# A transformer block of three stages on one core: the length penalty added by TensorE in PSUM, one maximum over four banks, exponentials out of PSUM, and ranks by a difference and one compare

## The reference

```python
# part 1, per batch: self attention, then cross attention over a context of 2048 rows
Q = x @ Wq2
K, V = (context @ Wk2, context @ Wv2)
energy = einsum('bqd,bkd->bqk', Q, K)
lengths = sum(energy[:, 0] != 0, axis=-1)       # how many keys the first query does not meet with 0
pad = arange(2048) >= lengths
energy = where(pad, -inf, energy)
score = softmax(energy / sqrt(32), axis=-1)
# ... then a two-layer feed-forward, a layer norm after each step
# part 2: an RWKV step over the two batches
# part 3, per batch: attention with gates
gl_v = (x @ Ws).reshape(b, t, h, e)              # 8 heads, 5 experts
wv = topk_mask(gl_v, 2) * sigmoid(gl_v)          # the two highest; the lower index wins a tie
xv = einsum('btd,edk->btek', x, Wv)
v = einsum('bthe,btek->bhtk', wv, xv)
# ... softmax(q k) v, gated by topk_mask(x @ Wd, 2), through Wo
```

## Time and profile before

| | |
|---|---|
| median of 3 runs | 277.52 us (277.33 to 278.31) |
| span of the profiled execution | 275.8 us |
| PE busy | 237.3 us, 86% of the span |
| DVE busy | 177.9 us, 64% |
| ACT busy | 88.3 us, 32% |
| POOL busy | 99.6 us, 36% |
| chain that ended last | PE 54%, DVE 29%, POOL 5%, issue 5%, ACT 4% |

### The profile page before, as it was taken

How to read it: one execution, slowest core, us unless ns; L and a number is a source line. 1 busy time by engine, 2 the same in 40 slices (tenths; PEclk the granted TensorE clock), 3 DMA queues, 4 the chain that set the end, 5 groups by cost and what they waited for, 6 DMA issues and landing times.

```text
span 275.8 us, 3044 instructions
## 1 busy us (share of the span) xinstructions
PE 237.3 (86%) x1133; PEld 167.4 (61%) x1133; DVE 177.9 (64%) x327; ACT 88.3 (32%) x151; POOL 99.6 (36%) x82
## 2 busy tenths in 40 slices
PE   6999869899599949999989999970987599996995
PEld 5969458789488727677554444430433279895952
DVE  2236953379658999540747559599646869899360
ACT  2106410363467538412014545410202302321110
POOL 4002810088039933530402024886215236160000
PEclk9999968999899997999999999997799979999579
DMA  6999991002799991009800797000000000000001
GB/s 269 394 421 450 409 422 76 1 0 101 289 429 421 421 424 51 0 11 392 358 2 1 221 421 311 1 0 0 0 0 0 2 0 0 4 0 0 2 37 40
DMA packets 6350, 43.98 MB, mean 159 GB/s; under 512 B 832, under 2 KB 832, under 8 KB 1472
## 3 DMA queue, kind: packets, MB, share of 16 engines
q1 hardware_dynamic: 6336, 43.80, 39.1%
HBM read 43.27 MB, written 0.52 MB: 159 GB/s over the span
## 4 chain that ended last, share of the span: by engine, by line
PE 54%; DVE 29%; POOL 5%; issue 5%; ACT 4%; DMA 1%; DVEq 0%; POOLq 0%; ACTq 0%
PE psum L378 50%; PE psum L382 4%; DVE ring_r L809 4%; ACT slots L1338 3%; POOL small L1576 3%; DVE slots L1078 3%; DVE slots L904 2%; POOL slots L1585 2%; DVE slots L1081 2%; DVE small L785 1%; DVE slots L978 1%; DVE slots L909 1%; DMA slots<-xin 1%; DVE small L1091 1%; DVE slots L998 1%
## 5 line engine op out<-in xcount | busy, mean ns | idle before, releaser
L378 PE MATMUL psum<-ring,slots 128*128 128x512 f32 (+3 forms) x228 | 96.2, 576 | 4.4 <-ACT slots L1338 4.4
L378 PEld LDWEIGHTS psum<-ring,slots 128*128 128x128 f32 (+1 forms) x228 | 43.2, 209 | 48.7 <-issue 41.5
L1338 ACT ACTIVATE slots<-psum 128x512 f32<-128x512 f32 (+3 forms) x51 | 27.7, 552 | 123.6 <-PE psum L378 76.2
L1581 POOL TENSOR_TENSOR ring_r<-ring,ring_r 128x640 fp32r<-128x640 f32 x16 | 41.5, 2608 | 48.5 <-ACT ring_r L1338 48.5
L378 PE MATMUL psum<-slots,ring 128*128 128x128 f32 x448 | 54.7, 283 | 2.9 <-ACT slots L1338 2.4
L378 PEld LDWEIGHTS psum<-slots,ring 128*128 128x128 f32 x448 | 53.5, 199 | 5.1 <-ACT slots L1338 3.4
L378 PE MATMUL psum<-ring_r,slots_r 128*128 128x512 f32 x192 | 48.4, 410 | 3.4 <-issue 3.4
L378 PEld LDWEIGHTS psum<-ring_r,slots_r 128*128 128x128 f32 x192 | 37.1, 196 | 12.6 <-issue 4.9
L1576 POOL TENSOR_TENSOR small<-small,mhalf 128x1 f32<-128x1 f32 x16 | 14.9, 932 | 62.2 <-DVE small L789 62.2
L1338 ACT ACTIVATE ring_r<-ring 128x2048 fp32r<-128x2048 f32 (+1 forms) x17 | 31.7, 1864 | 14.2 <-PE psum L378 12.6
L382 PE MATMUL psum<-ident,slots 128*128 128x128 f32 x104 | 17.1, 298 | 19.5 <-DVE slots L1274 7.9
(11 more groups left out here) (149 smaller groups left out, 211.1 us busy)
## 6 DMA issues: line engine op xcount, KB each, us to landing
ring<-blocks SPq DMA_DIRECT2D x36, 1024.0 KB, 10.2
bc<-vecs SPq DMA_DIRECT2D x1, 3072.0 KB, 28.4
bc<-vecs SPq DMA_DIRECT2D x1, 1280.0 KB, 8.1
slots<-xin SPq DMA_DIRECT2D x2, 256.0 KB, 3.9
bc<-vecs SPq DMA_DIRECT2D x1, 512.0 KB, 9.9
y<-slots SPq DMA_DIRECT2D x2, 256.0 KB, 2.0
colv<-cols SPq DMA_DIRECT2D x1, 14.0 KB, 8.7
```

Of the source, the lines that this page charges most:

```text
L378: return t.matmul(o_, l, r, start=first, stop=last)
L1338: return a.activation(o, x, func, **kw)
L1581: g.tensor_tensor(ring_r[:, p, CUT:], ring[:, p, CUT:], ring_r[:, high(name), CUT:], ALU.subtract).then_inc(*split_lowg.inc(name))
```

## The change

- The penalty is no longer a 128x512 tile for each bank. `penalty(b)` on VectorE makes one 4x512 tile (one row for each bank, from an index that counts on over the rows and the length in PSUM), and `shut_out(b)` on TensorE adds it to the four banks with four matmuls of a 4x128 picker.
- `count2` adds the four counts up in one PSUM column: four matmuls of one column each, where there was one of four columns.
- `maxima` is one reduction over the four banks and one scaling.
- `exp2` is two exponentials of 1024, read from PSUM; in batch 1 both stand ahead of `gathered(0)`, where two stood behind `split("c12")`.
- `k2_split(1)` moves ahead of `maxima(0)`; `guard` moves to directly behind the penalty.
- `ranks` is a difference and one compare with a tie threshold (0, or minus the smallest normal number); GpSimd's `ties` is gone.
- The start-up constants change (index, picker and tie threshold for thresholds, `top` and triangle), and ScalarE copies the picker first of all. A bias row is multiplied by a 1x128 row of ones, where it was a 128x128 tile with one row of ones.

```diff
             def count2(b):
                 bk = 3 if b else 7
-                s.wait_ge(*counted[b].at("3"))
-                count(b, psum[:, bk, 0:4], cnt4[b][0:1, :], "n2")
+                for n in range(4):
+                    s.wait_ge(*counted[b].at(str(n)))
+                    i = mm(psum[:, bk, 0:1], ones[0:1, :], cnt4[b][0:1, n:n + 1], n == 0, n == 3)
+                i.then_inc(*prod[b].inc("n2"))
+
+            def shut_out(b):
+                s.wait_ge(*counted[b].at("pen"))
+                s.wait_ge(*sel_a.at("pick"))
+                for n in range(4):
+                    i = t.matmul(bank(4 * b + n), pick_r[:, n, :], pen_r[b], start=False, stop=True,
+                             skip_group_check=True)
+                i.then_inc(*shut[b].inc("pen"))
...
             def turn_p(b, n):
-                s.wait_ge(*exped[b].at(str(n)))
-                if n < 2:
-                    s.wait_ge(*maxed[b].at(str(n)))
-                else:
+                s.wait_ge(*exped[b].at(str(n // 2)))
+                if n > 1:
...
             k2(1)
+            shut_out(0)
             scores(1, 0)
...
             gather(0, 1)
+            shut_out(1)
             gather(0, 2)
...
-            def length2(b):
+            def penalty(b):
                 s.wait_ge(*prod[b].at("n2"))
...
+                s.wait_ge(*normed[b].at("x1"))
+                v.tensor_scalar(pen_r[b], kidx4[:, :], psum[0:4, 3 if b else 7, 0:1], NEG, ALU.is_ge,
+                                ALU.mult).then_inc(*counted[b].inc("pen"))
+                guard(b, psum[:, 3 if b else 7, 0:1])
 
             def maxima(b):
...
+                s.wait_ge(*shut[b].at("pen"))
+                v.tensor_reduce(mxp[b], psum[:, 4 * b:4 * b + 4, :], AX.XY, ALU.max).then_inc(*maxed[b].inc("max"))
+                s.wait_ge(*maxed[b].at("max"))
+                v.tensor_scalar(nb2[b], mxp[b], -SC, None, ALU.mult).then_inc(*maxed[b].inc("nb2"))
...
-                v.tensor_tensor(r1, other, mine, ALU.is_equal).then_inc(*gates_v[b].inc("eq"))
-                v.tensor_tensor(r0, other, mine, ALU.is_gt).then_inc(*own_v.inc())
-                s.wait_ge(*own_v.now())
-                s.wait_ge(*rank_g[b].at("tri"))
-                v.tensor_tensor(r0, r0, r1, ALU.add).then_inc(*own_v.inc())
+                s.wait_ge(*const.at("tie"))
+                v.tensor_tensor(r0, other, mine, ALU.subtract).then_inc(*own_v.inc())
+                s.wait_ge(*own_v.now())
+                v.tensor_tensor(r0, r0, tie[:, :, :].unsqueeze(1).broadcast_to([128, 16, 5, 5]),
+                                ALU.is_gt).then_inc(*own_v.inc())
...
             low("ct12")
-            length2(0)
+            penalty(0)
+            k2_split(1)
             maxima(0)
-            k2_split(1)
-            neg_max(0)
-            guard(0, len2[0])
             weigh2(0)
...
             low("c02")
-            length2(1)
+            penalty(1)
             low("c03")
             maxima(1)
-            neg_max(1)
...
+            def exp2(b, q):
                 s.wait_ge(*maxed[b].at("nb2"))
-                act(e, e, ACT.Exp, bias=nb2[b], scale=SC, accum_out=sm2[b][:, n:n + 1]).then_inc(
-                    *exped[b].inc(str(n)))
+                act(Em[b][:, q * 1024:(q + 1) * 1024].rearrange("p (n k) -> p n k", n=2),
+                    psum[:, 4 * b + 2 * q:4 * b + 2 * q + 2, :], ACT.Exp, bias=nb2[b], scale=SC,
+                    accum_out=sm2[b][:, q:q + 1]).then_inc(*exped[b].inc(str(q)))
...
             split("c12")
-            exp2(1, 2)
-            exp2(1, 3)
             copy_turned(0, "pc", T16, 3)
...
-            g.memset(top[:, :], 0.0).then_inc(*own_g.inc())
+            g.iota(kidx4[:, :], pattern=[[1, 512]], base=0, channel_multiplier=512,
+                   allow_small_or_imprecise_dtypes=True).then_inc(*const.inc("kidx4"))
+            g.memset(pick, 0.0).then_inc(*own_g.inc())
             s.wait_ge(*own_g.now())
-            g.memset(top[0:1, :], 1.0).then_inc(*const.inc("top"))
+            g.affine_select(out=pick, in_=pick, compare_op=ALU.not_equal, fill=1.0, base=0,
+                            pattern=[[-1, 4], [0, 128]], channel_multiplier=1).then_inc(*const.inc("pick"))
```

More of the change, by code:

```diff
@@ L151, in vec @@
             return bc[:, i if i < FIRST_BC else i - FIRST_BC, :]
+        pick = slots[0:4, 36, :].rearrange("p (n m) -> p n m", n=4)
+        pick_r = slots_r[0:4, 37, :].rearrange("p (n m) -> p n m", n=4)
+        pen_r = [slots_r[0:4, 34 + b, :] for b in range(2)]
         X = [slot(0), slot(1)]
@@ L198, in build @@
         lo1, re1, gd = (cells(1) for _ in range(3))
[L199 removed]
+        cnt4, len2, mxp, nb2, sm2, s1, rv2 = (cells(n) for n in (4, 1, 1, 1, 2, 1, 1))
         ss, sbs, mu8, ssq, rs8 = (cells(8) for _ in range(5))
@@ L229, in build @@
         k2_low = flags("k2_low", ["k2"])
-        counted = flags("counted", four + ["len2"])
-        maxed = flags("maxed", four + ["nb2"])
+        counted = flags("counted", four + ["pen"])
+        maxed = flags("maxed", ["max", "nb2"])
         p_low = flags("p_low", four)
@@ L246, in build @@
                       ["q1", "v1", "q2", "k2", "pc", "relu", "k", "th", "w", "r", "v", "g"])
-        exped = flags("exped", ["e1"] + four)
+        exped = flags("exped", ["e1", "0", "1"])
         split_high = Flag(sem("split_high"), SPLITS)
@@ L275, in build @@
         score = flags("score", four)
+        shut = flags("shut", ["pen"])
         p_turn = flags("p_turn", four)
@@ L400, in bias @@
             def bias(name, bk):
-                s.wait_ge(*const.at("top"))
-                mm(bank(bk), top[:, :], vec(name), True, False)
+                mm(bank(bk), ones[0:1, :], vec(name)[0:1, :], True, False)
             def natural(b, name, src, bk, what, width=512, on_bias=False):
@@ L890, in nonzero @@
                                 ALU.add, accum_out=cnt4[b][0:1, n:n + 1]).then_inc(*counted[b].inc(str(n)))
-            def length2(b):
+            def penalty(b):
                 s.wait_ge(*prod[b].at("n2"))
[L894 to L897, removed]
-            def maxima(b):
[L900 to L905, removed]
-                    s.wait_ge(*own_v.now())
-                    if n:
-                        s.wait_ge(*maxed[b].at(str(n - 1)))
-                    v.tensor_tensor_reduce(out=Em[b][:, at_], in0=bank(4 * b + n), in1=PT[b][:, at_], scale=1.0,
-                                           scalar=mxp[b][:, n - 1:n] if n else NEG, op0=ALU.add, op1=ALU.max,
-                                           accum_out=mxp[b][:, n:n + 1]).then_inc(*maxed[b].inc(str(n)))
-            def neg_max(b):
-                s.wait_ge(*maxed[b].at("3"))
-                v.tensor_scalar(nb2[b], mxp[b][:, 3:4], -SC, None, ALU.mult).then_inc(*maxed[b].inc("nb2"))
+                s.wait_ge(*const.at("kidx4"))
+                s.wait_ge(*normed[b].at("x1"))
+                v.tensor_scalar(pen_r[b], kidx4[:, :], psum[0:4, 3 if b else 7, 0:1], NEG, ALU.is_ge,
+                                ALU.mult).then_inc(*counted[b].inc("pen"))
+                guard(b, psum[:, 3 if b else 7, 0:1])
+            def maxima(b):
+                s.wait_ge(*shut[b].at("pen"))
+                v.tensor_reduce(mxp[b], psum[:, 4 * b:4 * b + 4, :], AX.XY, ALU.max).then_inc(*maxed[b].inc("max"))
+                s.wait_ge(*maxed[b].at("max"))
+                v.tensor_scalar(nb2[b], mxp[b], -SC, None, ALU.mult).then_inc(*maxed[b].inc("nb2"))
             def p_split(b, n):
@@ L1202, in _ @@
             p_split(1, 1)
-            guard(1, len2[1])
             low("c12")
@@ L1423, in fk_out, with pickers @@
                 act(bcols(T16, b), quarters(4 * b), ACT.Copy).then_inc(*gates_a[b].inc("k"))
+            def pickers():
+                s.wait_ge(*const.at("pick"))
+                act(pick_r, pick, ACT.Copy).then_inc(*sel_a.inc("pick"))
             def select():
@@ L1476, in _ @@
             out(1, "k2", bcols(T12_r, 1), quarters(6))
-            for n in range(4):
-                exp2(0, n)
+            exp2(0, 0)
+            exp2(0, 1)
             split("ct13")
```

44 lines of the change are left out of this document (15 added, 29 removed).

## The result

| | before | after |
|---|---|---|
| median of 4 runs each, one chip | 277.42 us (275.56 to 278.31) | 268.41 us (267.33 to 269.15) |
| profiled execution, span | 277.5, 275.8 us | 268.02, 266.3 us |
| share of the chain, PE and DVE | 54% and 29% | 68% and 17% |

The ratio is 0.9676, with a 95% interval of 0.9617 to 0.9735: faster by 9.0 us, where 10.5 were forecast. The range (265 to 273) and the forecast's own range (265 to 269) both hold the time. A ratio leaves out executions over 1.5% above their kernel's fastest (a slower state), so where ratio and medians differ, the ratio is the one to read. As will be seen, the mechanisms of the sum came true, but one term that it puts at nothing is not nothing, and part of the nearness is luck.

What follows compares the result with a forecast made beforehand. TensorE's chain (54%) was taken to bound the kernel, with stalls of 3.00, 4.28 and 2.69 us and a lowered clock. Span 275.8 - 4.9 (scores) - 1.4 (ranks) - 4.2 (clock) = 265.3, median 1.7 above: 267.0 us, range 265 to 273.

Steps and rivals of the forecast that it cites:

- bias products: Start-up change: one-row bias products have as many columns as the 128-row ones, so they cost nothing.
- Batch 0 and 1: Scores: PE's stalls of 3.00 and 4.28 us shrink, turn_p(0, 0) 2.3 us and gather(1, 0) 4.5 sooner; 4.9 in all.
- Rival 2: Batch 1's stall stays as GpSimd's lows come late, costing 2 to 3 us: 269.5, or 273.7 without the clock; chance 0.14.
- Ranks: Batch 1's ranks on VectorE: two dependent operations take 1.22 us in place of 2.60, so turn_max(1) comes 1.4 us sooner.
- Clock of the last part: From turn_max(1) on: idle ahead falls from 2.69 to 1.25 us, the clock stays up, 19.8 us become 15.3; 4.2 counted.
- Rival 1: The last part's clock falls all the same, from VectorE's gap and the small products behind it: 271.2 us; chance 0.25.
- Rivals 3: The scores' change gives nothing, the saved time being a wait on something else; only 1.4 from ranks: 276.0 us; chance 0.05.
- rival 4: Slower: a contraction over 4 rows takes several passes, up to 7.4 us for a shut_out: 283.7 us; chance 0.04.

Runs made afterwards that it cites:

- before_row: The kernel before with only its bias products changed, to contract one row in place of 128: 280.44 us against 276.88, ratio 1.0122.
- after_top: The kernel after with only the bias products taken back to 128 rows: 266.39 us against 276.88 for before, ratio 0.963.
- scores_top: The kernel after with the old ranks and the 128-row bias products of before: 272.63 us against 277.44 for before, ratio 0.9858.
- ranks_only: The kernel before with only the new ranks: 270.93 us against 276.88, ratio 0.9776.
- best: The kernel after with 128-row bias, one four-column count product, split("c11") behind batch 1's exponentials, v2(0) ahead of gather(1, 1): 264.23 us against 277.44 for before.
- before_fill: The kernel before with eight unused 128 x 128 products in front of turn_max(1): 272.36 us against 277.44, ratio 0.9821.
- scores_only: The kernel after with the ranks of before: 275.10 us against 276.88 for before, ratio 0.9894.
- rows_stream: The kernel after with unused 512-column fp32 products at its end, 16 each over 128, 1, 4, 32, 64, 128 rows; run once: 398.16 us.
- rows_mixed: The kernel after with unused 512-column fp32 products at its end, 16 each over 128, 64, 128, 96, 128, 32, 128 rows; run once: 372.85 us.

## Why the prediction was right, and where it was not

The lead of after over before on PE, in the profiled executions, says which term of the sum came true. After was 1.35 us ahead at the first count (64.37 against 65.72 in the earlier trace rows), before any part of the change has begun to work: the idle ahead of the products at 36 us was 2.24 us and not 3.09, and behind it the clock was low for 3.4 us and not 6.8. The other traces show that this is scatter between executions and not the change: with the start of before, the first count stands at 64.08 (before_row), 65.18, 65.25 and 65.27 us, and with the start of after at 64.11 (after_top), 64.77, 65.16, 65.34, 65.43 and 65.54. It is taken off in the first two rows.

| step | forecast | measured |
|---|---|---|
| turn_p(0, 0) sooner, from the first count | 2.3 us | 2.16 (74.22 against 77.73, less 1.35) |
| gather(1, 0) sooner, likewise | 4.5 | 4.00 (101.22 against 106.57, less 1.35) |
| four banks' maximum, exponential of 1024 | 2.3, 1.15 | 2.28, 1.11 |
| count2, shut_out | 1.1, 0.95 | 1.05, 1.19 |
| bias products | nothing | 8.83 against 7.13 us behind them |
| lead at fg(1) | 4.9 | 3.26 (231.38 against 234.64), 1.35 of it from the start |
| from fg(1) to turn_max(1) | 1.4 | 1.43 |
| from turn_max(1) to PE's last matmul | 4.2 | 4.81 (14.99 against 19.80) |
| span | 10.5 | 9.5, with the 1.35 |

**Batch 0 and 1.** Right in mechanism and nearly in size. The clock was kept over gaps of 0.34 and 0.57 us as foreseen, and the long stalls went. The half microsecond missing in batch 1 is the count and shut_out, which the sum had at 1.6 us more than before. The count now holds PE for 0.98 us from its start to the next (87.05 to 88.03), where it held it for 0.31 (90.55 to 90.86 in before); and gather(0, 1) to gather(0, 3) with shut_out between them take 9.80 us (88.03 to 97.83), where before's 36 matmuls, without a break, took 8.45. That is 2.0 us more. That GpSimd holds such operations was in the forecast (1.8 us), and the trace agrees: 1.79 for the penalty and 1.15 for the 128 x 1 product. The Trainium skill, "SBUF — State Buffer", section "Who interferes with whom", has VectorE locked out by GpSimd's use of a shared port pair when it reads two operands in SBUF, which fits the product, or works in a two-port mode; of the penalty's mode no row tells. Neither was on the path. Rival 2, a stall that stays, is out: the gap at 98.27 is 0.44 us.

**"The bias products have as many columns as before: nothing."** This is the step that failed. The four passes themselves take 1.98 us against 1.88, but the clock falls 1.4 us behind their end (at 143.5) and costs 1.7 us there; the one edit alone made the kernel before 3.4 us slower in before_row. I had counted columns and looked for the clock only where PE stands, as in the earlier trace rows. The step is wrong even though two of five traces escape the fall.

The lead of after falls from 5.99 us at the last gather (116.61 against 122.60) to 3.26 at fg(1), and 1.7 of these 2.7 us are lost behind the bias products. The rest are changes of the clock behind gaps that the change did not touch, and they go both ways. After's clock rises sooner behind the long gap at 180 us (its lead grows from 3.98 us at 188.52 to 4.63 at 198.61), and is low for longer at 215 to 222: fg(0) takes 5.70 us where it took 4.57. No run isolates these two. This is a second thing that the sum had at nothing: it carries a lead to the end unchanged. In scores_top 1.9 us of the 4.85 were lost behind such gaps.

**Ranks.** Right: 1.43 us to turn_max(1).

**Clock of the last part.** Right: the idle is 1.27 us (forecast 1.25), and the clock stays. Rival 1, a fall in spite of the short gap, is out: in all six traces with an idle of 1.27 us there, after, ranks_only, after_top and best among them, the clock stays up. That it is the idle and not the ranks, before_fill shows. The size is 0.6 us more than forecast, since I held back a wait on ACT that did not come.

**Rivals 3 and 4.** The scores do give something without the ranks, 2.9 us in scores_only and 3.9 in scores_top, each with an interval clear of nothing. A matmul over 4 rows costs 0.30 us and not the 1.1 from which rival 4 would have decided.

So the nearness of the forecast is in part luck. In the span of the profiled execution (9.5 us of gain against 10.5) the fall behind the bias products (1.7) was left out, and against it stand 0.6 too little in the last part and 1.35 us of lead that the change did not make; without this lead the gain would have been some 8.2, an estimate from these figures.

## What to carry to other kernels

Read the granted clock beside every gap of TensorE: shortening one gap from 2.69 to 1.27 us gave 1.4 us of time and 4.8 of clock, and useless products in the gap gave 5.1. An edit of TensorE's operands is not free because its columns are the same: a contraction over one row in place of 128 took the clock down for the work behind it in three of five traces, and the edit by itself cost 1.2% of this kernel. Do not carry a saved microsecond to the end of a kernel as it is: behind unchanged gaps the lower level lasted 3.4 us longer in one trace than in another. And where one engine's order is changed to remove a stall, ask what else it still has to do: with 4.8 us of maxima left, the stall and its fall of the clock only moved.

## What the runs showed of the hardware

- The clock fell while PE was busy without a gap, when its fp32 products of 512 columns contracted over few rows: at 281.6 us of rows_stream (one row, in a block from 276.1) and at 337.9 of rows_mixed (32 rows, from 332.8). Over 64 rows it stayed at the level it had, 0.50 in one run and 1.00 in the other; over 96 rows, behind a block at full clock, it was 1.00; and in the blocks over 128 rows that began at the lower level it rose, at 384.0 and 358.4.
- Behind four passes over one row, 1.98 us in all, the clock fell to the lower level in after (0.57 in 143 to 147 us), before_row and rows_mixed, and stayed at 1.00 in scores_only and rows_stream.
- From 12 us on, the twelve traces have 49 idles of PE of 2.2 to 7.9 us, and the lower level came behind the start of each, for 3.4 to 13.7 us. It came behind none of the eighteen of 1.23 to 1.27 us. Of three of about 1.46 us it came behind one: in before_fill, from 38.7 us on (0.84 in the mean of 36 to 40), where in rows_mixed the same gap left 1.00.
- A VectorE maximum over four banks of PSUM (2048 elements) took 2.28 us in one instruction; ACT's exponential of 1024 from PSUM 1.11.
- Fp32r matmuls of 512 columns took no longer over 4 rows than over 128: 12 over 128 rows show as 3.00 us and 36 as 8.45, that is 0.227 us each and 0.28 once, by which four come to some 1.2; the four over 4 rows took 1.19.
